# A transformer block with a graph layer: roots spread through a DRAM row, probabilities normalised ahead of their transposes, the mix by features

## What is computed

```python
# layer 1: 16 heads of 16 features
x_mod = rms(x) * (1 + scale_msa) + shift_msa          # first norm, "norm 0"
q, k, v = split(x_mod @ qkv_w); q, k = rope(rms(q)), rope(rms(k))
attn = softmax(q @ k.T / 4)                            # 64 x 64 a head
x = x + gate_msa * (attn @ v @ proj_w + proj_b)
h = rms(x) * (1 + scale_mlp) + shift_mlp               # second norm, "norm 1"
x = x + gate_mlp * (silu(h @ w1_w) * (h @ w3_w) @ w2_w)    # 704 hidden features
# layer 2: graph attention over the first 20 rows, two directions
self_feat = concat(x, cond or 0) @ W_self.T + b_self   # 0 where a row of x sums to 0
w = softmax(where(edges > 0, q1 @ k1.T / 4, -9e15) + edge_bias)
out = x + relu(self_feat + sum over directions of (w @ kv) @ Wout + bout)
```

## Time and profile before

| | us |
|---|---|
| median of 3 runs (lowest, highest) | 1424.35 (1419.06, 1425.61) |
| the profiled execution, its span | 1418.18, 1416.1 |
| PE busy, share of the span | 1342.2, 95% |
| DVE | 1135.2, 80% |
| ACT | 878.6, 62% |
| POOL | 712.1, 50% |

### The profile page before, as it was taken

How to read it: one execution, slowest core, us unless ns; L and a number is a source line. 1 busy time by engine, 2 the same in 40 slices (tenths; PEclk the granted TensorE clock), 3 DMA queues, 4 the chain that set the end, 5 groups by cost and what they waited for, 6 DMA issues and landing times.

```text
span 1416.1 us, 51305 instructions
## 1 busy us (share of the span) xinstructions
PE 1342.2 (95%) x20276; PEld 1229.1 (87%) x20276; DVE 1135.2 (80%) x2033; ACT 878.6 (62%) x1752; POOL 712.1 (50%) x612
## 2 busy tenths in 40 slices
PE   4679999999999999999999999999999999999985
PEld 3578899999998999999898999999999999999974
DVE  5667888888888888888888888888888888888753
ACT  4556666666666666666666666666666666656542
POOL 0235555455655544555555455555545555554541
PEclk8589999999999999999999999999999999999998
DMA  7001111010111101111110111111011111100100
GB/s 240 29 23 30 45 43 43 18 38 30 43 43 43 43 15 36 34 43 43 43 43 15 35 35 43 43 43 43 15 33 37 43 43 43 43 15 28 30 22 16
DMA packets 49827, 56.19 MB, mean 40 GB/s; under 512 B 4352, under 2 KB 47744, under 8 KB 49792
## 3 DMA queue, kind: packets, MB, share of 16 engines
q1 hardware_dynamic: 48944, 53.86, 12.1%
q10 hardware_dynamic: 848, 1.84, 0.4%
HBM read 47.03 MB, written 8.65 MB: 39 GB/s over the span
## 4 chain that ended last, share of the span: by engine, by line
PE 73%; issue 9%; POOL 7%; ACT 3%; DVE 1%; ACTq 0%; POOLq 0%; DVEq 0%
PE psum L486 39%; PE psum L607 5%; PE psum L622 5%; PE psum L728 4%; PE psum L792 4%; PE psum L758 4%; PE psum L775 3%; POOL nl L1315 3%; PE psum L587 3%; PE psum L806 2%; POOL gl L1315 2%; POOL kbd L1327 2%; ACT gh L926 1%; PE psum L534 1%; ACT qkT L892 1%
## 5 line engine op out<-in xcount | busy, mean ns | idle before, releaser
L1315 POOL TENSOR_TENSOR gl<-gf,gh 128x512 fp32r<-128x512 f32 x96 | 124.3, 1295 | 260.4 <-ACT gh L926 260.4
L486 PE MATMUL psum<-nh,w_lo 128*128 128x256 f32 x704 | 182.2, 289 | 0.0
L486 PE MATMUL psum<-nh,w_hi 128*128 128x256 f32 x704 | 176.8, 282 | 0.0
L1315 POOL TENSOR_TENSOR nl<-xn,nh 128x512 fp32r<-128x512 f32 x64 | 99.2, 1551 | 127.3 <-ACT nh L864 127.3
L486 PEld LDWEIGHTS psum<-nh,w_lo 128*128 128x128 f32 x704 | 132.8, 189 | 1.0 <-issue 1.0
L486 PEld LDWEIGHTS psum<-nh,w_hi 128*128 128x128 f32 x704 | 133.0, 189 | 0.0
L1379 POOL TENSOR_TENSOR e<-e,inv 128x640 f32<-128x640 f32 x64 | 82.0, 1282 | 87.6 <-DVE inv L1271 87.6
L486 PE MATMUL psum<-nl,w_hi 128*128 128x256 f32 x704 | 115.4, 282 | 0.0
L926 ACT ACTIVATE gh<-gf 128x512 fp32r<-128x512 f32 x96 | 60.3, 628 | 61.6 <-DVE gf L1201 60.8
L486 PEld LDWEIGHTS psum<-nl,w_hi 128*128 128x128 f32 x704 | 97.5, 188 | 0.0
L486 PE MATMUL psum<-qkv_lo,nh 128*128 128x512 f32 (+1 forms) x256 | 88.5, 356 | 2.8 <-ACT nh L864 2.8
(11 more groups left out here) (186 smaller groups left out, 4382.4 us busy)
## 6 DMA issues: line engine op xcount, KB each, us to landing
adj<-in_adj SPq DMA_DIRECT2D x32, 440.0 KB, 3.3
x_in<-in_x SPq DMA_DIRECT2D x32, 256.0 KB, 2.7
xn<-in_xT SPq DMA_DIRECT2D x32, 256.0 KB, 3.6
x_res<-in_xT SPq DMA_DIRECT2D x32, 256.0 KB, 3.7
out_T<-y SPq DMA_DIRECT2D x32, 256.0 KB, 2.2
e<-in_adaln ACTq DMA_DIRECT2D x2, 512.0 KB, 5.4
stage<-in_qkv SPq DMA_DIRECT2D x2, 384.0 KB, 5.0
pT<-in_w SPq DMA_DIRECT2D x2, 384.0 KB, 6.4
```

The costliest lines, as they stand in the source:

```text
L486: last = nc.tensor.matmul(out, lhsT, rhs, start=start and i == 0, stop=stop and i == len(terms) - 1)
L1315: return nc.gpsimd.tensor_tensor(out, full, hi.bitcast(F32), ALU.subtract)
```

## The change

The first norm's inverse roots are stored by SP as a row of 256 values in DRAM and loaded back on all partitions (`inv0_all`); PE's two transposes go. The sum, its reciprocal and the product with it are made on the exponentials of layer 1, by DVE and POOL, ahead of their transposes; the columns of ones go. `mix` takes the form of layer 2's, writes features on partitions, and the transposes back (`mixT` on PE) go; ACT and DVE split its result as before. The transposed probabilities are written over the exponentials' own tile, and those of layer 2 get a tile per t. The last 64 hidden features: the low part of g is put on the idle lower half of `gh`, and w2's last 64 rows are there twice, so that two products of 128 rows an output chunk take the place of three of 64. `gate` and `cond_rows` get 128 rows, zeros below the eighth. The edge bias is added in one instruction a tile. All orders and banks are new; the condition's split, the sine tables and two low parts of weights move behind the first shift on DVE.

```diff
     "PE": [
-        (2, "heads", 1), (1, "proj", 0), (0, "self", 0), (0, "self_cond", 0), (2, "score", 0), (0, "k1", 0),
-        (0, "q1", 0), (1, "norm1_mean", 0), (0, "q1", 1), (1, "norm1_apply", 0), (2, "probsT", 0),
-        (3, "norm0_apply", 0), (0, "score1", 0), (0, "v1", 0), (2, "mix", 0), (2, "probsT", 1), (1, "mlp_up", 0),
-        (1, "mlp_up", 1), (3, "qkv", 0), (0, "probsT1", 0), (2, "mix", 1), (3, "qkv", 1), (0, "mix1", 0),
-        (0, "probsT1", 1), (1, "mlp_up", 2), (0, "mix1", 1), (1, "mlp_down", 0), (1, "mlp_down", 1), (2, "mixT", 0),
-        (3, "heads", 0),
+        (2, "mix", 0), (2, "probsT", 1), (3, "qkv", 0), (2, "mix", 1), (1, "mlp_up", 2), (3, "qkv", 1),
+        (0, "probsT1", 0), (1, "mlp_down", 0), (0, "probsT1", 1), (0, "mix1", 0), (0, "mix1", 1), (1, "mlp_down", 1),
+        (3, "heads", 0), (3, "heads", 1), (2, "proj", 0), (1, "self", 0), (1, "self_cond", 0), (3, "score", 0),
+        (1, "k1", 0), (2, "norm1_mean", 0), (1, "q1", 0), (2, "norm1_apply", 0), (1, "q1", 1), (1, "v1", 0),
+        (1, "score1", 0), (2, "mlp_up", 0), (3, "probsT", 0), (2, "mlp_up", 1),
     ],
     "DVE": [
-        (2, "rope", 0), (2, "rope", 1), (0, "mlp_down", 0), (1, "mixT", 0), (1, "proj", 0), (0, "row_mask", 0),
-        (0, "edge_masks", 0), (2, "score_max", 0), (2, "score", 0), (1, "norm1_squares", 0), (2, "score_max", 1),
-        (1, "norm1_mean", 0), (0, "k1", 0), (2, "score", 1), (1, "norm1_apply", 0), (1, "norm1_shift", 0),
-        (3, "norm0_apply", 0), (3, "norm0_shift", 0), (0, "score1_bias", 0), (0, "score1_max", 0),
-        (0, "score1_bias", 1), (0, "score1", 0), (2, "mix", 0), (0, "score1_max", 1), (0, "soft1", 0),
-        (0, "soft1_inverse", 0), (1, "mlp_up", 0), (0, "score1", 1), (0, "soft1", 1), (0, "soft1_inverse", 1),
-        (1, "mlp_up", 1), (2, "mix", 1), (3, "qkv", 0), (3, "qkv", 1), (1, "mlp_up", 2), (0, "mix1", 0),
-        (1, "edges", 0), (3, "rope_scale", 0), (0, "out", 0),
+        (1, "norm1_mean", 0), (2, "score_max", 1), (2, "score", 1), (1, "norm1_apply", 0), (0, "k1", 0),
+        (1, "norm1_shift", 0), (2, "soft0", 0), (2, "soft0_inverse", 0), (2, "soft0", 1), (0, "score1_bias", 0),
+        (0, "score1_bias", 1), (0, "score1_max", 0), (2, "soft0_inverse", 1), (3, "norm0_apply", 0), (0, "score1", 0),
+        (1, "mlp_up", 0), (0, "score1_max", 1), (3, "norm0_shift", 0), (0, "score1", 1), (0, "soft1", 0),
+        (0, "soft1_inverse", 0), (1, "edges", 0), (0, "soft1", 1), (1, "mlp_up", 1), (0, "soft1_inverse", 1),
+        (3, "qkv", 0), (1, "mlp_up", 2), (3, "qkv", 1), (1, "edge_masks", 0), (3, "rope_scale", 0), (3, "rope", 0),
+        (0, "mix1", 0), (3, "rope", 1), (0, "out", 0), (1, "mlp_down", 0), (2, "mixT", 0), (2, "proj", 0),
+        (1, "row_mask", 0), (3, "score_max", 0), (2, "norm1_squares", 0), (3, "score", 0),
     ],
     "Activation": [
-        (2, "rope_scale", 0), (0, "mlp_split", 2), (1, "mixT", 0), (2, "heads", 0), (2, "heads", 1),
-        (0, "x2_split", 0), (0, "self", 0), (1, "norm1_mean", 0), (0, "keys", 0), (0, "self_split", 0),
-        (3, "norm0_mean", 0), (2, "score", 0), (0, "q1", 0), (0, "q1", 1), (2, "probsT", 0), (2, "score", 1),
-        (1, "norm1_apply", 0), (0, "v1", 0), (3, "norm0_apply", 0), (1, "edges", 0), (0, "score1", 0),
-        (2, "probsT", 1), (1, "mlp_up", 0), (1, "mlp_split", 0), (0, "score1", 1), (1, "mlp_up", 1),
-        (0, "probsT1", 0), (3, "qkv", 0), (1, "mlp_split", 1), (3, "qkv", 1), (0, "probsT1", 1), (1, "mlp_up", 2),
+        (2, "heads", 0), (0, "x2_split", 0), (2, "heads", 1), (0, "self", 0), (0, "keys", 0), (1, "norm1_mean", 0),
+        (0, "self_split", 0), (3, "norm0_mean", 0), (2, "score", 0), (0, "q1", 0), (0, "q1", 1), (2, "score", 1),
+        (1, "norm1_apply", 0), (1, "mlp_up", 0), (1, "edges", 0), (2, "probsT", 0), (0, "score1", 0), (0, "v1", 0),
+        (1, "mlp_up", 1), (1, "mlp_split", 0), (3, "norm0_apply", 0), (0, "score1", 1), (2, "probsT", 1),
+        (3, "qkv", 0), (1, "mlp_split", 1), (1, "mlp_up", 2), (2, "mixT", 0), (3, "qkv", 1), (0, "probsT1", 0),
+        (1, "mlp_split", 2), (3, "rope_scale", 0), (0, "probsT1", 1),
     ],
     "Pool": [
-        (1, "proj", 0), (0, "self_split", 0), (3, "norm0_mean", 0), (1, "norm1_mean", 0), (1, "norm1_scale", 0),
-        (3, "norm0_scale", 0), (1, "norm1_apply", 0), (3, "norm0_apply", 0), (0, "soft1", 0), (1, "mlp_up", 0),
-        (0, "soft1", 1), (1, "edges", 0), (1, "mlp_up", 1), (1, "mlp_up", 2), (1, "mlp_down", 0), (3, "heads", 0),
-        (1, "x2_split", 0), (3, "heads", 1),
+        (1, "proj", 0), (1, "norm1_scale", 0), (0, "self_split", 0), (1, "norm1_mean", 0), (3, "norm0_mean", 0),
+        (3, "norm0_scale", 0), (1, "norm1_apply", 0), (2, "soft0", 0), (2, "soft0", 1), (3, "norm0_apply", 0),
+        (1, "mlp_up", 0), (0, "soft1", 0), (1, "mlp_up", 1), (0, "soft1", 1), (1, "edges", 0), (1, "mlp_up", 2),
+        (1, "mlp_down", 0), (3, "heads", 0), (1, "x2_split", 0), (3, "heads", 1),
     ],
     "SP": [
-        (0, "self", 0), (3, "norm0_mean", 0), (1, "mlp_up", 0), (3, "norm0_scale", 0), (2, "norm0_apply", 0),
-        (0, "out", 0),
+        (3, "norm0_mean", 0), (2, "norm0_apply", 0), (3, "norm0_scale", 0), (3, "norm0_root", 0), (1, "self", 0),
+        (3, "norm0_spread", 0), (2, "mlp_up", 0), (0, "out", 0),
     ],
 }
```

```diff
+            def store_roots(m, n):
+                wait(sp, inverses[0], m, 1)
+                sp.dma_start(inv_rows[bass.ds(m, 1), :].rearrange("m (t p) -> p (m t)", p=P), rms_inv[0][:, :], allow_slow_non_contiguous=True).then_inc(inv_rows_s.sem, 16)
+
+            def load_roots(m, n):
+                wait(sp, inv_rows_s, m, 16)
+                sp.dma_start(inv0_all[:, :], inv_rows[bass.ds(m, 1), :].to_broadcast([P, MT])).then_inc(inv_all_s.sem, 16)
...
-            def norm0_apply(m, n):
-                wait(pe, inverses[0], m, 1)
-                wait_free(pe, m, (q1_kept, -3, 2), (mixed_lo, -2, 1), (normed[0], -1, 1))
-                for t in range(TILES):
-                    last = nc.tensor.transpose(spread0_ps[:, t * P:(t + 1) * P],
-                                               rms_inv[0][:, t:t + 1].to_broadcast([P, P]), ident[:, :])
-                last.then_inc(spread[0].sem, 1)
...
-                        last = nc.tensor.matmul(mix_ps[t][s * S:(s + 1) * S, j, :], pT0[:, j, s * S:(s + 1) * S],
-                                                vb[:, t, s, j, :], start=True, stop=True, tile_position=(0, s * S))
+                        f = 32 * (j % 4)
+                        last = nc.tensor.matmul(mix_ps[f:f + 32, j // 4, t * P + s * S:t * P + (s + 1) * S],
+                                                vb[:, t, s, j, :], pT0[t][:, j, s * S:(s + 1) * S],
+                                                start=True, stop=True, tile_position=(0, f))
                 last.then_inc(mixed.sem, 1)
-
-            def mix_t(m, n):
-                wait(pe, mix_normed, m, TILES)
-                wait_free(pe, m, (z_silu, -1, 3), (mix_normed, 0, 2))
-                for c in range(DC):
-                    for t in range(TILES):
-                        last = nc.tensor.transpose(aoT_ps[:, c * MT + t * P:c * MT + (t + 1) * P],
...
-                    for i, (w, a) in enumerate(((wl["w2"], gh), (wh["w2"], gh), (wh["w2"], gl))):
-                        last = nc.tensor.matmul(down_ps[:, o, :], w[half, MC - 1, out_chunks[o]], a[half, MC - 1, :],
-                                                start=False, stop=o == DC - 1 and i == 2, tile_position=(HALF, 0))
+                    last = linear(down_ps[:, o, :], high_terms("w2", out_chunks[o], gh, [MC - 1]), False, o == DC - 1)
...
-                wait(dve, pT_ps, m, 2 * (t + 1 - TILES))
+                wait(dve, mixed, m, t + 1 - TILES)
...
-            def mix(m, t):
-                wait(dve, mixed, m, t + 1)
-                wait(dve, mix_normed, m, t + 1 - TILES)
-                nc.vector.reciprocal(inv0[t][:, :, :], mix_ps[t][:, :, 2 * DH:2 * DH + 2]).then_inc(inv_sums.sem, 1)
-                wait(dve, inv_sums, m, t + 1)
-                wait_last(dve, aoT_done, m)
-                nc.vector.tensor_tensor(aon[t][:, :, :, :], mix_ps[t][:, :, 0:2 * DH].rearrange("p j (h f) -> p j h f", h=2),
-                                        inv0[t][:, :, :].unsqueeze(3).to_broadcast([P, NJ, 2, DH]), ALU.mult)\
-                    .then_inc(mix_normed.sem, 1)
+            def soft0(m, t):
+                wait(dve, exps, m, t + 1)
+                wait(dve, inv_sums, m, t)
+                nc.vector.tensor_reduce(sum0[:, :], e0[t][:, :, :], AX.X, ALU.add).then_inc(sums0.sem, 1)
+
+            def soft0_inverse(m, t):
+                wait(dve, sums0, m, t + 1)
+                nc.vector.reciprocal(inv0[t][:, :], sum0[:, :]).then_inc(inv_sums.sem, 1)
 
...
-                for a in range(ND):
-                    nc.vector.tensor_tensor(
-                        e1[t][:, :, a, 0:NKV].rearrange("p (r h) k -> p r h k", r=NG),
```

(32 more changed lines are left out.)

226 lines of the change are left out of this document (115 added, 111 removed).

## The result

The changed kernel takes 1655.38 us (median of 4 runs, 1650.63 to 1657.92), the kernel before 1423.18 in the same comparison: a ratio of 1.1631, with a 95% interval of 1.1592 to 1.1671, so 232 us slower. The prediction said 1446, with a range up to 1482. Its sign was right, its size was not: a turn of the loop takes about 48.5 us and not 42.3.

What follows compares the result with a forecast made beforehand. DVE was to become the bound: cycle 41.21 us plus 1.05 for meeting POOL, 42.26 a turn, +0.87 over 29 turns, +25 on 1418.2 makes 1443, plus 3 for the median: 1446 us; range 1392 to 1482.

Steps and rivals of the forecast that it cites:

- The DRAM row: First norm's roots through DRAM: two transfers, at most 8.2 us, hidden behind 8 us of cover; cost 0, up to +2.
- the other estimate there: Store and load of the roots, by the Trainium skill's fixed some 2 us a transfer: the pair lands in about 4.
- rival 4: Roots late at the first norm: past 8 us of transfers each us costs 29; at 9.5 us 1490; chance 0.06.
- PE's terms: TensorE's work a turn: transposes, mix, half-height products and self_cond save 2.0 us, so PE would need 39.4.
- The cycle: One turn is at least the window plus DVE's work outside it: 38.85 us before, 41.21 after, held to 40.5 to 41.8.
- The window: Stretch from DVE's gate multiply to its score maximum that no order can shorten: 7.31 us, shortened by self_cond's 0.10.
- The two row sums: Sums of 128x1024 added on DVE: 1.14 us each by the nearest operation of that size, 2.28 together.
- Who gets in DVE's way: DVE and POOL block each other when both combine two SBUF operands; +1.05 us a turn, bounds 0 and 1.3.
- Squares: DVE step directly behind the first score maximum: meets POOL's self_split and starts 1.05 us late.
- The cycle without meetings: Window plus DVE's work outside it, before any delay from POOL: 41.21 us a turn.
- rival 3: POOL's product gets between DVE's norm0_apply and score1: 1.3 to 2.05 us a turn more, 1484 to 1505; chance 0.10.
- The masks: DVE's edge_masks move out of the window, where DVE would idle, to between qkv and rope_scale: +1.69 us a turn.

Runs made afterwards that it cites:

- the version without the row: Changed kernel, but the first norm's roots go back through two TensorE transposes, with no DRAM store or load: 1487.83 us, ratio 1.0472.
- the two later runs: Roots through TensorE, masks back, SyncE's order mended: with MLP products ahead of DVE's subtraction, 1463.53 us; with norm sooner and rotation pair moved apart, 1436.16 us.

## Why the prediction was wrong, point by point

**The DRAM row: the step that failed.** The prediction asked whether the roots come in time, priced the store by the slowest row of the loop and put it at 0 to +2 a turn. As a size that was wrong, 8.3 + 4.8 = 13.1 us instead of at most 8.2 (or of about 4, the other estimate there), past the two usual lengths that it allowed the scattered one. As lateness it hardly shows, 1.4 us of DVE's waiting a turn (rival 4 would have charged 5), since the engines ahead of norm0_apply had stopped as well. What the prediction never asked is what the store does to others while it lands. Taking the store out gives back 142 of the 232 us, which the stops on issue and the slower clock behind them account for, and the same store costs 191 us in the kernel before with no reader at all. The earlier trace rows could not show it: every transfer of the loop there moves long pieces. The range should have taken a bound from outside those rows. The Trainium skill (DMA: Bandwidth & Descriptors, Specifications) names 512 bytes as the limit below which pieces are read, modified and written; that covers 8-byte and 4-byte pieces alike and so would not have told them apart, where the runs show 11 against 191 us for 256 of each.

**PE's terms: right.** 2.0 us less than the 41.12 of the earlier trace rows, plus 0.43 for the transposes that came back in the version without the row, is 39.5; it shows 39.45. Mix products took 0.69 us a tile, under the 0.81 taken.

**The cycle: right in form.** The window from the gate multiply to the score maximum is 7.16 us in that version (720.74 to 727.90), against 7.21 forecast. DVE has no wait of note outside it, so window and work make the turn, as said. The two row sums cost 1.24 and 1.14 us from start to start (735.39 to 736.63, 736.99 to 738.13), as taken. It is a bound and not the only one: with 1.4 and 1.7 us a turn less of DVE's work, in the two later runs, the turn did not move.

**Who gets in DVE's way: wrong meeting, low price.** Squares was to lose 1.05 us and lost nothing: POOL's self_split comes behind it. What met were the subtraction, 2 x (1.51 - 0.82) = 1.4 us, and the rotation pairs, 4 x (0.87 - 0.57) = 1.2. The cycle without meetings, 41.21, and these make 43.8; the turn is 43.65. The first of them is rival 3, POOL's product between norm0_apply and score1, priced at 1484 to 1505: the version without the row takes 1488. It had a chance of 0.10 because DVE was expected to keep its turn; POOL begins 0.16 us after norm0_apply does and gets the next one. That 1488 lies in rival 3's range is in part luck: the range stands on top of the 1.05 us for squares, which did not come, and lacks the rotation pairs, which did. And the price of a meeting is read from DVE's lengths here, not from a run: taking the first one away gave nothing where it was tried.

**The masks: right in sign.** Forecast +1.69 a turn; the turn falls by 0.98 us (43.65 to 42.67) when they go back, 24 us in two pairs of runs. In the late place the three take 1.42 us from start to start (759.40 to 760.82), and 0.4 us comes back as DVE's wait for PE ahead of the last layer's sum (7.0 us in 19 turns).

**Sum.** Of +232: the store 142, the load and the factor in SBUF 24, DVE's work, meetings and orders 66. Only the last was in the forecast, as 25. Of the 66, runs give back 24 with the masks and some 30 with the norm sooner; 13 are left. So without the store the time would still lie above the range (1488 and 1512 against 1482), by DVE's meetings and by a norm that comes late for QKV, which no term had.
